# Order of the constants, a buffer of its own for the first image's position parts, and a split over the used columns

## The reference

```
x = x + conv(_gn(x))          # _gn: group norm over 4 channels x all places of an image
    v      = xn @ v_w + v_b                                   # 8 groups of 32 channels
    deform = (xn @ qd_w + qd_b + prior) * sigmoid(xn @ qs_w + dscale) * 6
    w      = xn @ qw_w + qw_b                                 # 9 sample points per place and group
    samp   = bilinear sample of v at (place + deform), zero outside the image
    out    = (sum over the 9 points of w * samp) @ out_w + out_b
t = t + attention(layer norm(t))                              # 8 heads, 32 slices, 1024 tokens
t = t + experts(layer norm(t))                                # router, 2 of 8 experts, 512 hidden
```

## Time and profile before

| | us |
|---|---|
| median of 3 runs (lowest, highest) | 1552.92 (1536.53, 1554.06) |
| the profiled execution's own time | 1547.26 |
| its span, first to last instruction | 1544.8 |
| busy PE / DVE / ACT / POOL | 1215.9 / 904.8 / 733.5 / 693.5 |
| TensorE's mean granted clock, share of 2.4 GHz | 0.796 |

### The profile page before, as it was taken

The page is one execution under the profiler, slowest core; times in us unless marked ns, Lnnn a source line. Parts: engine busy times, 40 slices in busy tenths (PEclk is TensorE's granted clock), DMA queues, the critical chain, the costliest instruction groups (busy, mean ns, idle before and its releaser), DMA issues.

```text
span 1544.8 us, 63235 instructions
## 1 busy us (share of the span) xinstructions
PE 1215.9 (79%) x28236; PEld 943.8 (61%) x28236; DVE 904.8 (59%) x1619; ACT 733.5 (47%) x1403; POOL 693.5 (45%) x674
## 2 busy tenths in 40 slices
PE   3297785987898789998977889998877899865391
PEld 2165564665556568886565668875565688735291
DVE  4468578686768556446767454457785644464311
ACT  1255363553565256665553347665543566422060
POOL 4155455454443564347533744466335644420303
PEclk9568695795897668997996569997977899986596
DMA  5502213122000321552111224621103235200761
GB/s 137 136 25 52 79 40 78 60 58 79 25 27 22 88 83 58 149 146 68 30 35 44 68 69 124 182 86 42 38 11 98 73 108 163 83 18 0 243 178 53
DMA packets 166288, 121.96 MB, mean 79 GB/s; under 512 B 45641, under 2 KB 146050, under 8 KB 165506
## 3 DMA queue, kind: packets, MB, share of 16 engines
q1 hardware_dynamic: 161922, 109.53, 25.3%
q0 software_dynamic: 4096, 8.40, 1.8%
HBM read 89.38 MB, written 28.51 MB: 76 GB/s over the span
## 4 chain that ended last, share of the span: by engine, by line
PE 61%; DVE 21%; issue 8%; POOL 5%; ACT 2%; DMA 1%; SPq 0%; DVEq 0%; POOLq 0%; ACTq 0%
PE ps L743 15%; PE ps L758 14%; PE ps L731 7%; PE ps L918 5%; PE ps L931 5%; DVE asb L1339 4%; PE ps L766 3%; DVE yr L1331 2%; POOL ysb L655 1%; DVE x_tok L1348 1%; POOL picked L633 1%; DVE region L1297 1%; PE ps L787 1%; PE ps L841 1%; PE ps L696 1%
## 5 line engine op out<-in xcount | busy, mean ns | idle before, releaser
L655 POOL TENSOR_TENSOR ysb<-yr,rw 128x512 f32<-128x512 f32 x512 | 552.5, 1102 | 629.7 <-DVE yr L1331 549.9
L743 PEld LDWEIGHTS ps<-xsb,ysb 36*64 36x64 f32 x16384 | 324.6, 160 | 148.0 <-issue 120.5
L743 PE MATMUL ps<-xsb,ysb 36*64 36x64 f32 x16384 | 363.7, 249 | 58.0 <-DVE x_tok L1348 34.2
L1339 DVE COPY asb<-ps 128x1024 f32<-128x1024 f32 x256 | 312.3, 1220 | 163.3 <-PE ps L743 161.6
L1041 ACT ACTIVATE xsb<-xr,pick 128x512 f32<-128x512 f32 x512 | 361.7, 764 | 4.4
L1331 DVE TENSOR_SCALAR yr<-ps 128x512 f32<-128x512 f32 x256 | 174.3, 681 | 223.0 <-PE ps L731 217.6
L758 PE MATMUL ps<-asb,vd 32*32 32x256 f32 x8192 | 212.2, 465 | 63.4 <-DVE asb L1339 50.7
L731 PE MATMUL ps<-spread_b,lp 97*128 97x512 bf16 x512 | 190.4, 452 | 57.4 <-DVE yr L1331 28.6
L1031 ACT ACTIVATE xr<-ps 128x512 f32<-128x512 f32 x256 | 152.0, 594 | 172.5 <-PE ps L731 172.0
L758 PEld LDWEIGHTS ps<-asb,vd 32*32 32x32 f32 x8192 | 153.5, 114 | 116.1 <-issue 88.0
L1048 ACT ACTIVATE osp<-ps 128x256 f32<-128x256 f32 x128 | 39.6, 402 | 274.8 <-PE ps L758 274.8
(11 more groups left out here) (232 smaller groups left out, 1097.4 us busy)
## 6 DMA issues: line engine op xcount, KB each, us to landing
ring<-in_L_ffn_W SPq DMA_DIRECT2D x154, 256.0 KB, 3.3
vd<-group_values SPq DMA_DIRECT2D x128, 128.0 KB, 2.7
asb<-in_L_ffn_W SPq DMA_DIRECT2D x30, 256.0 KB, 4.5
position_parts<-region SPq DMA_DIRECT2D x4, 1536.0 KB, 5.8
lp<-position_parts SPq DMA_DIRECT2D x96, 64.0 KB, 2.6
group_values<-region SPq DMA_DIRECT2D x32, 128.0 KB, 3.4
weight_rows<-region SPq DMA_DIRECT2D x4, 1024.0 KB, 4.3
rw<-weight_rows SPq DMA_DIRECT2D x32, 128.0 KB
```

The costliest lines, as they stand in the source:

```text
L655: pl.tensor_tensor(ysb[:, n % 2, pair * CHUNK:(pair + 1) * CHUNK, u, :], yr[:, k % 3, :, :], rw[:, ig % 2, u, first:first + CHUNK].rearran ...
L743: last = pe.matmul(o[:, :, NV * q:NV * q + NV], ysb[rows, n % 2, col, :, :].rearrange("p u y -> p (u y)"), xsb[rows, n % 2, col, :, :], st ...
L1339: dve.tensor_copy(asb[:, :, :, 2 * beta + pair, :].rearrange("p x i m -> p i x m"), ps[:, 2 * pair:2 * pair + 2, :].rearrange("p i (x m) - ...
```

## The change

- **POOL's constants** come in the order in which they are wanted: identity and `gn_avg` whole, the iotas, `vbias`, `spread_f` with its three selects, then the zeros of `place_flat` and `turn_flat`, a new memset of `parts_early` (6144 bf16 columns), the ones of `lp`, then the head masks. PE's transposes wait for 5 of them, DVE's `small_constants` for 8, ACT for `small_constants` 8.
- **DVE's constants**: `conv_constants` and the new function `spread_constants` (the part of `small_constants` that makes `spread_b`, `full_tiles`, `before_e`, with waits for 13 and 19) run behind the differences of image 0 (step 15), not ahead of its statistics. `find_places` of image 0 waits for 17 before its last step.
- **A buffer of its own**: the parts of image 0 go to `parts_early`, in columns 16 to 27 of `asb`; `split_places` of image 0 no longer waits for the stored values. The first copy to `asb` (`take`) waits until the parts are stored.
- **Used columns**: the subtractions run over 32 runs of 36 columns, 1152 in place of 2048, for all images; the copies to bf16 do so for image 0 alone.
- **Order**: the edge weights (step 19) run ahead of the split (17, 18) for all images. In the slots of a next image: edge weights at 17, split at 18 and 19 (before: split 17 and 18, edge weights 19), turning and its copies one slot earlier, SP's store of the parts one slot later and of the weights one earlier.
- **First places loaded first**: `load_group` is cut in two, and for group 0 of image 0 SP issues the three loads of `lp` ahead of the store of the turned weights.

```diff
--- before.py
+++ after.py
...
 PREP_SLOTS = 23
-PE_PREP = ((0, 0), (3, 2), (4, 3)) + tuple((7 + t, 4 + t) for t in range(NT)) + ((21, 13), (22, 14))
-ACT_PREP = ((0, 0), (4, 3), (15, 12), (21, 13), (22, 14))
+PE_PREP = ((0, 0), (3, 2), (4, 3)) + tuple((7 + t, 4 + t) for t in range(NT)) + ((20, 13), (21, 14))
+ACT_PREP = ((0, 0), (4, 3), (15, 12), (20, 13), (21, 14))
 DVE_PREP = (((1, 1), (3, 2), (5, 3), (6, 15)) + tuple((7 + t, 4 + t) for t in range(NT))
-            + ((15, 16), (16, 12), (17, 17), (18, 18), (19, 19)))
-SP_PREP = ((14, 11), (18, 12), (22, 14))
+            + ((15, 16), (16, 12), (17, 19), (18, 17), (19, 18)))
+SP_PREP = ((14, 11), (19, 12), (21, 14))
...
         row_diff = v_flat[:, 0:N]
-        parts = region[:, 0:PARTS * G * P].bitcast(BF16).rearrange("p (r n) -> p r n", r=PARTS)
+        parts_late = region[:, 0:PARTS * G * P].bitcast(BF16).rearrange("p (r n) -> p r n", r=PARTS)
...
+        parts_early = asb[:, 16:28, :, :, :].rearrange("p x i n m -> p (x i n m)").bitcast(BF16)\
+            .rearrange("p (r n) -> p r n", r=PARTS)
...
         X_BANK, Y_BANK = 4, 5
-        VB_CLEAR = 10
+        EARLY_CLEAR = 9
...
         tiles_loaded = (s.tiles_loaded_0, s.tiles_loaded_1, s.tiles_loaded_2)
+        def parts_of(b):
+            return parts_late if b else parts_early
+        def used(flat):
+            return flat.rearrange("p (m n) -> p m n", n=P // NI)[:, :, 0:AK]
...
                          t_in["L0_conv_out_w"].rearrange("(g c) o -> c g o", g=G), "conv")
-                sp.wait_ge(s.constants_made, VB_CLEAR)
+                sp.wait_ge(s.constants_made, EARLY_CLEAR)
...
                 sp.wait_ge(s.parts_ready, b + 1)
-                sp.dma_start(parts_dram[b].rearrange("r p n -> p r n"), parts).then_inc(s.parts_stored, 16)
+                sp.dma_start(parts_dram[b].rearrange("r p n -> p r n"), parts_of(b)).then_inc(s.parts_stored, 16)
...
-            def load_group(ig):
+            def load_places(ig):
...
                       .then_inc(parts_loaded[ig % 2], 16)
+            def load_weights_values(ig):
+                b, g = ig // G, ig % G
...
             store_parts(0)
+            load_places(0)
             store_rows(0)
-            load_group(0)
+            load_weights_values(0)
...
                 if ig + 1 < IMAGES_GROUPS:
-                    load_group(ig + 1)
+                    load_places(ig + 1)
+                    load_weights_values(ig + 1)
...
             pl.memset(gn_avg[:, :], 1.0 / GN_GROUP).then_inc(s.constants_made, 1)
-            pl.memset(head_mask[:, :], 1.0).then_inc(s.constants_made, 1)
-            pl.memset(head_pick[:, :], 0.0).then_inc(s.constants_made, 1)
-            pl.memset(vbias[:, :], 0.0).then_inc(s.constants_made, 1)
-            pl.memset(spread_f, 0.0).then_inc(s.constants_made, 1)
-            pl.iota(pos_i.rearrange("p d (t k) -> p (d t) k", t=NT), pattern=[[0, 2], [P, NT], [0, K]], base=0,
-                    channel_multiplier=1).then_inc(s.constants_made, 1)
-            pl.iota(row_i[:, :], pattern=[[0, 2]], base=0, channel_multiplier=1).then_inc(s.constants_made, 1)
-            pl.iota(grid_i, pattern=[[1, GRID]], base=0, channel_multiplier=0).then_inc(s.constants_made, 1)
-            pl.memset(lp[:, :, :, :, :].rearrange("p r b d n -> p (r b d n)"), 1.0).then_inc(s.constants_made, 1)
-            pl.wait_ge(s.constants_made, VB_CLEAR)
+            pl.wait_ge(s.constants_made, 2)
...
-            block_diagonal(gn_avg, GN_GROUP, 11)
+            block_diagonal(gn_avg, GN_GROUP, 3)
+            pl.iota(pos_i.rearrange("p d (t k) -> p (d t) k", t=NT), pattern=[[0, 2], [P, NT], [0, K]], base=0,
+                    channel_multiplier=1).then_inc(s.constants_made, 1)
+            pl.iota(row_i[:, :], pattern=[[0, 2]], base=0, channel_multiplier=1).then_inc(s.constants_made, 1)
+            pl.iota(grid_i, pattern=[[1, GRID]], base=0, channel_multiplier=0).then_inc(s.constants_made, 1)
+            pl.memset(vbias[:, :], 0.0).then_inc(s.constants_made, 1)
+            pl.memset(spread_f, 0.0).then_inc(s.constants_made, 1)
+            for r in range(PARTS):
+                pl.wait_ge(s.constants_made, 10 + r)
+                pl.affine_select(out=spread_f, in_=spread_f, compare_op=ALU.not_equal, fill=1.0, base=-SETS * r,
+                                 pattern=[[-1, SETS], [0, GRID]], channel_multiplier=1).then_inc(s.constants_made, 1)
...
             pl.memset(turn_flat, 0.0).then_inc(s.constants_made, 1)
-
-            for r in range(PARTS):
-                if r:
-                    pl.wait_ge(s.constants_made, 15 + r)
-                pl.affine_select(out=spread_f, in_=spread_f, compare_op=ALU.not_equal, fill=1.0, base=-SETS * r,
-                                 pattern=[[-1, SETS], [0, GRID]], channel_multiplier=1).then_inc(s.constants_made, 1)
-            block_diagonal(head_mask, DH, 18)
+            pl.memset(parts_early.rearrange("p r n -> p (r n)"), 0.0).then_inc(s.constants_made, 1)
+            pl.memset(lp[:, :, :, :, :].rearrange("p r b d n -> p (r b d n)"), 1.0).then_inc(s.constants_made, 1)
+            pl.memset(head_mask[:, :], 1.0).then_inc(s.constants_made, 1)
+            pl.memset(head_pick[:, :], 0.0).then_inc(s.constants_made, 1)
+            pl.wait_ge(s.constants_made, 19)
+            block_diagonal(head_mask, DH, 19)
...
                 if q:
-                    pl.wait_ge(s.constants_made, 20 + q)
+                    pl.wait_ge(s.constants_made, 21 + q)
...
-            pe.wait_ge(s.constants_made, 13)
+            pe.wait_ge(s.constants_made, 5)
...
                 prepare(0, step)
-            pe.wait_ge(s.constants_made, 24)
+            pe.wait_ge(s.constants_made, 25)
...
         def _(act):
-            act.wait_ge(s.small_constants, 9)
+            act.wait_ge(s.small_constants, 8)
...
                 dve.memset(eps_col[:, :], EPS).then_inc(s.small_constants, 1)
-                dve.wait_ge(s.constants_made, 18)
+                dve.wait_ge(s.constants_made, 8)
...
+            def spread_constants():
+                dve.wait_ge(s.constants_made, 13)
...
                 dve.tensor_copy(spread_b[:, :, :], spread_f).then_inc(s.grid_chain, 2)
+                dve.wait_ge(s.constants_made, 19)
...
                 chain(s.position_chain, last, 3 * b + 2)
+                if b == 0:
+                    dve.wait_ge(s.constants_made, 17)
...
-                if half == 0:
+                if half == 0 and b:
                     dve.wait_ge(s.values_stored, 16 * G * (b + 1))
+                left = used(place_flat)
...
                         continue
-                    chain(s.split_chain, dve.tensor_copy(parts[:, r, :], place_flat), 5 * b + 2 * r + 1)
+                    taken = used(parts_of(b)[:, r, :])
+                    chain(s.split_chain, dve.tensor_copy(parts_of(b)[:, r, :], place_flat) if b else
+                          dve.tensor_copy(taken, left), 5 * b + 2 * r + 1)
                     if r < PARTS - 1:
-                        chain(s.split_chain, dve.tensor_tensor(place_flat, place_flat, parts[:, r, :], ALU.subtract),
-                              5 * b + 2 * r + 2)
+                        chain(s.split_chain, dve.tensor_tensor(left, left, taken, ALU.subtract), 5 * b + 2 * r + 2)
...
                     dve.wait_ge(s.out_summed, ig)
+                    if ig == 0:
+                        dve.wait_ge(s.parts_stored, 16)
...
             small_constants()
-            conv_constants()
...
                 prepare(0, step)
+                if step == 15:
+                    conv_constants()
+                    spread_constants()
```

## The result

| | before | after |
|---|---|---|
| median of 17 runs each, us (lowest, highest) | 1541.79 (1529.65, 1554.06) | 1524.60 (1518.24, 1533.16) |
| span of the profiled execution | 1544.8 | 1520.2 |
| mean granted clock in it | 0.796 | 0.806 |

The ratio is 0.9899, 95% interval 0.9879 to 0.9919: 15.6 us of 1541.79, between 12.5 and 18.7. The medians alone are 17.2 apart. The gain is within 2% and clear of no change. The forecast was 13.5 us less, its time 1534 with a range of 1516 to 1549.

What follows compares the result with a forecast made beforehand. Woven groups were bounded by a chain with PE 61% and DVE 21%; before first products, waits are paid in full. Join 8.5, opening 0 and woven 5 made 13.5 off 1547.26: 1534 us, range 1516 to 1549.

Steps and rivals of the forecast that it cites:

- the woven term: Images woven behind the start: narrower subtractions and edge weights hidden in image 1 gain 5 us, bounds 1 and 8.
- opening, up to the first tile: Start to first tile emptied: POOL's memsets hold DVE, so gain 0, bounds -1.5 and +7.1.
- tiles and places: From the first tile to the places' end: no gain counted, 0.
- join, places to `lp`'s issue: From the places to the issue of `lp`'s loads: 14.3 against 22.85, a gain of 8.5 us.
- from `lp`'s issue to the distances: From issuing `lp`'s loads to the first distances: kept at 4.9 us, low bound 3.9, no gain counted.
- rival 1: Opening: POOL's long memset doesn't hold DVE, so the opening adds 7.1 and the time is 1527 us; chance 0.20.
- the signs that I named: Profile: normalising 3+, little copy 1.5+, subtraction 1.36, first tile 26 to 28.5, distances 60 to 62, products 7.7 later.
- The sign against the forecast: Behind the first distances: forecast wrong if group times differ by more than 5 us in sum at equal clock.
- the forecast course: Opening: normalising runs 17.5 to 18.3 between two POOL memsets, then little copy waits until 20.1; first tile 27.0.
- Rival 2: Before first products: turned weights late, POOL starts 3 to 5 late, woven gain low; 1542 us; chance 0.14.
- Rival 3: Last image's expert tail: PE at the low clock level costs up to 39.6; 1550 us at 30; chance 0.06.

Runs made afterwards that it cites:

- e3: The change without the memset of the early parts buffer, image 0's copies over all 2048 columns; ratio to before 0.9879, first products at 60.43.
- e4: The change with the memset of 6144 columns cut into three pieces with a wait between; first tile at 22.48, no ratio.
- e2: The change with images 1 to 3 subtracting over all 2048 columns again; ratio to before 0.9930, first products at 64.75.
- e5: The change with SP's old order, store of the turned weights ahead of the first places' loads; ratio to before 0.9903, first products at 64.89.
- e6: The change with image 0's split waiting for the stored values again; first distances at 57.34, no ratio.
- e12: The change itself, unaltered, run again on another chip; ratio to before 0.9905, first products at 64.13.
- e7: The change with the old order of steps and slots for all images, split ahead of edge weights; ratio to before 0.9906, first products at 61.97.
- e8: The change with the old slots for images 1 to 3 only, image 0 in the new order; ratio to before 0.9875, first products at 63.25.
- e9: The change with both the old step and slot order and SP's old order; first products at 66.67, no ratio.
- e1: The kernel before with only the split's subtractions narrowed to the used columns, all images; ratio to before 0.9992, first products at 74.66.
- e10: The change without the early parts memset, whole-column copies for image 0, `lp`'s memset behind the head masks' selects; ratio to before 0.9916, first products at 61.33.
- e11: The change with ACT writing the early parts' zeros instead of POOL, `lp`'s memset behind the head masks' selects; ratio to before 0.9858, first products at 59.56.

## Why the prediction was right

The direction and the place were right: most of the gain is made ahead of the first products, where nothing is woven. The size was right in part by luck: the terms ahead of the first products were 4.8 too low in sum (8.5 for 13.3), the woven term 2.7 too high, and the two errors nearly cancel. By terms of the sum:

| term | forecast | measured |
|---|---|---|
| opening, up to the first tile | 0 | 1.6 |
| tiles and places | 0 | 1.1 |
| join, places to `lp`'s issue | 8.5 | 8.8 |
| from `lp`'s issue to the distances | 0 | 1.85 |
| woven images and all behind | 5 | 15.6 - 13.3 = 2.3 (-0.8 to 5.4) |
| sum | 13.5 | 15.6 (12.5 to 18.7) |

The forecast time, 1534, lies 9.2 above the measured median, and 5.5 of that is its base: I took the one profiled run, 1547.26, and the median of 17 is 1541.79. The measured 1524.60 is in fact nearer to rival 1's 1527 than to my 1534; what rules rival 1 out is not the time but the profile. Of the signs that I named, three came: the normalising of 3 us or more, products 7.7 behind the distances, 1.36 for a subtraction. Three did not: a little copy of 1.5 or more (0.18), a first tile at 26 to 28.5 (25.52), first distances at 60 to 62 (56.06). The sign against the forecast, group times at equal clock, can't be read, as the profiled clocks differ (0.796 and 0.806).

**The opening.** The step that decided was whether POOL's long memset holds DVE. It does (e3, e4); without it the opening gains 6.6 (e3: first tile 20.52 for 27.08), and rival 1 falls. What the section "Who interferes with whom" of the page "SBUF — State Buffer" in the Trainium skill says, whoever starts first blocks the other for the whole instruction, agrees with 6.38 against 1.32 and 0.81 as far as a memset in front of one DVE instruction goes. The size came out near for partly wrong reasons. I let DVE and POOL take turns one by one. But the small constants were faster (done at 7.6, forecast 9.5): several DVE instructions held by `spread_f`'s memset ended together at 4.5, so ACT was not held. And DVE did not get its turn between the two memsets: forecast 17.5 to 18.3 for the normalising and then a wait of the little copy, measured one wait to 19.73 and a copy of 0.18. At the copy's end the two courses meet: 20.1 forecast, 19.95 measured. In eight profiles of the unchanged opening the normalising took 6.4 to 6.7 in five (the change, e2, e5, e6, e12) and 4.6 to 4.9 in three (e7, e8, e9). The three are the kernels with the old slot tables, though what DVE and POOL do up to there is the same in all eight; two profiles of one kernel, the change and e12, agree. What decides whether DVE gets in between two memsets that are queued back to back stays open. In the three the forecast course came true: normalising to 17.85, the little copy of 1.74 to 19.6. Yet the first tile was at 24.25 and not at 27.0, because the subtraction behind the copy ran under the memset, as in e4; that overlap the forecast lacked. The 1.1 in tiles and places is PE's: the fast pace of the tiles set in with the third, before with the fourth. It is no effect that a run shows: the stretch took 13.4 to 14.2 in the same eight profiles, 14.5 before and 14.0 in e1, whose code there is that of before.

**The join.** Edge weights 3.5, split 5.2, store 5.3: as forecast. The copies in gaps kept the fast rate (0.76, forecast 0.75), the subtraction 1.36 as forecast. The mis-sized term is `lp`'s landing: I kept 4.9 and set 3.9 as the low bound, it is 3.05 with no store in front of it. e5, with the store in front but nearly through, has 3.7, e9 again 4.9. The weights were late by nothing: POOL started 8.4 behind `lp`'s issue, forecast at most 10.0. Rival 2 falls. What the forecast did not see is how much the parts cover for each other: the values wait (e6), SP's order (e5) and the step order (e7) are each worth about 1 us or less alone; the last two together 3.4.

**The woven images.** The local forecast was too low, the lasting one too high. DVE copies the products of each batch into `asb`, so these copies are a clock for the woven work; the preparation of image 1 ends around the 16th to 25th. Times between their starts, us, in all 14 profiles:

| kernels (narrow: subtraction over the used columns) | 1st to 16th | 16th to 25th | 25th to 65th | 1st to 65th |
|---|---|---|---|---|
| before: old order, whole subtraction | 60.7 | 54.9 | 195.5 | 311.1 |
| e1, e7, e8, e9: old order, narrow | 58.8 to 60.8 | 50.9 to 53.6 | 187.8 to 194.7 | 299.0 to 309.0 |
| e2: new order, whole | 60.3 | 46.8 | 197.1 | 304.1 |
| the change, e3, e4, e5, e6, e10, e11, e12: new order, narrow | 59.0 to 61.3 | 45.0 to 49.4 | 191.5 to 202.0 | 298.0 to 307.4 |

The first column moves by the level of PE's granted clock: from the 1st to the 5th copy eight profiles took 12.0 us at a granted clock of 0.50 and six 10.4 to 10.8 at 0.78 to 0.81, and kernels with the same start (the change and e12 against e2 and e8) are in both groups. From the 16th to the 17th copy, a slot with one half of the split, before has 16.9, e1 15.0: 1.8 for the narrow subtraction there. The order is worth more than I had put: among the narrow kernels the mean from the 16th to the 25th falls from 52.4 to 46.7, 5.7 us, where I had 2 to 3 for order and subtraction in image 1 together, and no profile of either order lies in the other's range. But from the 25th to the 65th the mean rises from 190.2 to 196.8, and from the 1st to the 65th nothing is left of it (302.6 and 303.3). So the gain of the order is given back behind image 1, which is why e8 loses nothing at the end.

Part of both is the granted clock. It averages 0.74 with the old order and 0.79 with the new from the 16th to the 25th, and 0.77 and 0.75 behind that. How much of the return is the clock and how much are waits that the shorter slot uncovers, no run separates. And single executions differ by more than the gain. The stretch from the 17th to the 65th copy (windows: us, then busy PE, PEld, DVE, ACT, POOL, granted clock, DMA, GB/s), before:

```profile
156.70:390.20 233.50, 187.05 (x4927) 138.97 (x4928) 163.99 (x204) 113.25 (x186) 113.77 (x95) 0.74 0.23 66
```

After, and e12, the same kernel:

```profile
137.30:372.30 235.00, 190.86 (x4926) 140.72 (x4926) 161.64 (x201) 113.53 (x187) 112.51 (x96) 0.74 0.23 66
...
138.00:373.40 235.40, 193.27 (x4930) 142.98 (x4929) 161.72 (x201) 113.71 (x187) 112.61 (x96) 0.72 0.23 66
```

e6, whose woven code is the change's:

```profile
139.00:365.00 226.00, 182.03 (x4927) 135.32 (x4928) 161.79 (x201) 113.21 (x187) 112.71 (x96) 0.77 0.24 69
```

e8 and e9, with the old order:

```profile
140.30:366.20 225.90, 180.31 (x4926) 133.87 (x4926) 160.77 (x205) 112.64 (x186) 111.04 (x95) 0.77 0.24 69
...
143.90:367.70 223.80, 179.98 (x4927) 133.02 (x4928) 160.46 (x205) 112.67 (x186) 111.07 (x95) 0.77 0.25 69
```

The change and e6 run the same code here and differ by 9.0 us, and the mean granted clock, 0.74 against 0.77, goes with the length. A local gain of 3 to 6 us is thus smaller than what the share of the two clock levels, 1.2 and 2.4 GHz, moves between executions. These profiles are of several chips. Up to the 65th copy the chips do not show (before 311.1 and e1 309.0 are of a fast and a slow one); they part at the end, from the 128th copy to the last with 637 to 642 us on the two faster chips and 658 to 675 on the others.

Rival 3's mechanism, the low level in the last image's experts, did not come in the profiled run: the last nine slices of the granted clock on the page read 899986596 in both profiles. The two runs of the change that were profiled have 1520.2 and 1528.1 as spans with the same start to 0.4 us.

## What to carry to other kernels

Ahead of the first woven work every wait is paid in full, and events there repeat within 1.5 us, so that is where a few microseconds can be both won and proved; in the woven part a local gain must be larger than what the granted clock moves, and it must be followed further than the stretch in which it is made: here 5.7 us of it were gone 40 copies later. When waits in a join are removed one by one, look for which of them covers which: here three edits that are each worth about nothing alone, two of which hold 3.4 us between them. And add up the errors of a forecast term by term before trusting a sum that came out near. A constant that nobody needs yet is not free on an idle engine: a long memset in POOL's queue stalls each fast copy of DVE behind it, and if it must be there, cut it up with a wait between the pieces, or give it to ACT, which wrote the same zeros beside DVE without holding it (e11).

## What the runs showed of the hardware

- A POOL memset of 6144 bf16 columns (5.22 us) holds a DVE `tensor_scalar` SBUF to SBUF until its end, and with another memset queued back to back through both in five profiles (6.4 to 6.7) and only through the first in three (4.6 to 4.9). In those three the second memset took 2.35 in place of 1.80: the hold goes both ways. With a semaphore wait between pieces DVE gets in at once (1.16).
- Several DVE instructions that stand behind such a hold end within 0.1 us of each other (at 4.45 to 4.53 in the profile after), not one per turn.
- A DVE subtraction with two inputs in SBUF overlaps a memset (e4: done together with the held copy in front), but two of POOL's selects that began under such a subtraction lasted 1.28 and 1.24 in place of 0.32 and 0.39. What in the two operations makes the difference, these runs do not separate.
- ACT's three copies of 2048 columns (5.5 us, e11) ran beside DVE's 0.81 without any hold.
- With PE at the low level (0.50) from the first to the fifth batch of image 0, this stretch took 12.0 us in eight profiles; at 0.78 to 0.81 it took 10.4 to 10.8 in six, with the same code in both groups.
